# Eight in place of four output tiles scaled by ScalarE and added in DRAM, and a third tile's statistics on ScalarE

## The reference, cut to what matters

```python
x = x + gnn(_layernorm(x), edge_index, W, b)                # 1250 x 1024, 20000 edges
x = x + ffn(_layernorm(x)[None], router_w, ..., ln_w, ln_b)[0]

# inside ffn: hidden_states is the second layer norm's result, 8 experts, 2 of them for each row
for e in range(n_exp):
    y = jax.nn.gelu(flat @ w1[e].T + b1[e], approximate=False)
    y = y @ w2[e].T + b2[e]
    out = out + y * cw[:, None]
out = out.reshape(b, s, h) + hidden_states
return _layernorm(out, ln_w, ln_b)       # (out - mu) * rsqrt(var + 1e-12) * w + b
```

## Time and profile before

| | us |
|---|---|
| median of 3 runs | 693.21 |
| lowest, highest | 691.17, 694.19 |
| time of the profiled execution | 693.42 |
| its span, first to last instruction | 691.7 |
| outside the span | 1.7 |

### The profile page before, as it was taken

The page is one execution under the profiler, slowest core; times in us unless marked ns, Lnnn a source line. Parts: engine busy times, 40 slices in busy tenths (PEclk is TensorE's granted clock), DMA queues, the critical chain, the costliest instruction groups (busy, mean ns, idle before and its releaser), DMA issues.

```text
span 691.7 us, 13064 instructions
## 1 busy us (share of the span) xinstructions
PE 569.9 (82%) x3923; PEld 318.6 (46%) x3924; DVE 495.7 (72%) x1323; ACT 247.5 (36%) x374; POOL 221.8 (32%) x208
## 2 busy tenths in 40 slices
PE   1688999999999999996495999999999988999400
PEld 0243455445444554443383465646565645655100
DVE  8998977776227799999977867675767572363387
ACT  4322433233325234343442434443344341221280
POOL 2730000000000356867636343434343432041231
PEclk9999999999989999999598999999999995999855
DMA  5693000000006423333655787878787878050878
GB/s 197 243 374 122 3 1 1 1 2 2 1 2 231 172 93 147 126 150 122 203 170 181 203 271 179 284 182 281 174 273 184 264 198 309 0 81 13 196 240 262
DMA packets 35052, 106.15 MB, mean 153 GB/s; under 512 B 8978, under 2 KB 9391, under 8 KB 34992
## 3 DMA queue, kind: packets, MB, share of 16 engines
q1 hardware_dynamic: 24912, 73.86, 28.6%
q0 software_dynamic: 8896, 27.38, 18.8%
q10 hardware_dynamic: 1184, 4.20, 2.0%
HBM read 71.75 MB, written 33.67 MB: 152 GB/s over the span
## 4 chain that ended last, share of the span: by engine, by line
PE 55%; DVE 31%; issue 6%; DMA 4%; ACT 1%; DVEq 1%; POOL 1%; POOLq 0%; ACTq 0%; SPq 0%
PE ps L1863 6%; PE ps L1865 6%; PE ps L1864 6%; PE ps L1825 5%; PE ps L1826 5%; PE ps L1827 5%; PE ps L1657 4%; PE ps L1658 3%; PE ps L1659 3%; PE ps L1807 3%; PE ps L1603 2%; DVE last_ends L1328 2%; DVE wbufs L1143 2%; DVE oh_all L1022 2%; DVE wbufs L1246 2%
## 5 line engine op out<-in xcount | busy, mean ns | idle before, releaser
L606 POOL DMA_INDIRECT acc_rows<-work,ids_out x24 | 47.8, 1990 | 134.1 <-DVE work L1464 134.1
L511 POOL TENSOR_TENSOR work<-work 128x1024 f16<-128x1024 f32 x9 | 19.1, 2128 | 217.0 <-ACT work L872 217.0
L1825 PE MATMUL ps<-rows_and_counts,wbufs 128*128 128x336 f16 (+1 forms) x256 | 75.3, 299 | 9.0 <-DVE rows_and_counts L1406 5.6
L1417 DVE SCALAR_TENSOR_TENSOR wbufs<-stage,wbufs 128x1024 f16<-128x1024 f32 x56 | 67.1, 1218 | 12.6 <-ACT wbufs L899 12.6
L1733 PE MATMUL ps<-wbufs,rows_and_counts 128*128 128x512 f16 x200 | 75.8, 379 | 0.5 <-DVE wbufs L1246 0.5
L1734 PE MATMUL ps<-wbufs,rows_and_counts 128*128 128x512 f16 x200 | 75.8, 379 | 0.0
L1826 PE MATMUL ps<-rows_and_counts,wbufs 128*128 128x336 f16 (+1 forms) x256 | 75.3, 299 | 0.0
L1827 PE MATMUL ps<-rows_and_counts,wbufs 128*128 128x336 f16 (+1 forms) x256 | 75.2, 299 | 0.0
L1863 PE MATMUL ps<-wbufs,rows_and_counts 128*128 x192 | 73.4, 382 | 1.4 <-issue 1.4
L1864 PE MATMUL ps<-wbufs,rows_and_counts 128*128 x192 | 73.3, 382 | 0.0
L1865 PE MATMUL ps<-wbufs,rows_and_counts 128*128 x192 | 73.3, 382 | 0.0
(11 more groups left out here) (307 smaller groups left out, 1176.6 us busy)
## 6 DMA issues: line engine op xcount, KB each, us to landing
stage<-wst_in SPq DMA_DIRECT2D x72, 512.0 KB, 6.3
acc_rows<-work SPq DMA_DIRECT2D x10, 512.0 KB, 2.6
x_rows<-work SPq DMA_DIRECT2D x10, 512.0 KB, 2.6
t<-x_in SPq DMA_DIRECT2D x1, 4096.0 KB, 14.1
wbufs<-b_in ACTq DMA_DIRECT2D x8, 512.0 KB, 6.3
wbufs<-acc_rows SPq DMA_DIRECT2D x8, 512.0 KB, 6.2
t<-x_in SPq DMA_DIRECT2D x1, 3072.0 KB, 10.2
t<-x_in SPq DMA_DIRECT2D x1, 2048.0 KB, 7.8
```

The lines of the kernel that those rows point to most:

```text
L1825: mm(o, wbufs[:, ds(w + ws, P)], x_hi, start=(j == 0), stop=False)
```

## The change

Tiles 4 to 7 move from `WHOLE` to `ADDED`, and tile 2 moves from VectorE's statistics to ScalarE's.

```diff
-ACT_TILES = (0, 1), (4, 5), (8,)
-ADDED = LAST_GROUPS[0]
-WHOLE = LAST_GROUPS[1] + LAST_GROUPS[2]
+ACT_TILES = (0, 1, 2), (4, 5), (8,)
+ADDED = LAST_GROUPS[0] + LAST_GROUPS[1]
+WHOLE = LAST_GROUPS[2]
```

## The result

| | before | changed |
|---|---|---|
| median, us | 693.7 (4 runs) | 706.21 (4 runs) |
| lowest to highest, us | 691.17 to 694.43 | 704.0 to 708.72 |
| span of the profiled execution, us | 691.7 | 707.0 |

The ratio is 1.0187, 95% interval 1.0158 to 1.0217: the change costs about 13 us. (Each ratio in this document compares a kernel with runs of the kernel before that were taken together with it.) I had forecast 699.0, with a range up to 702.0. The sign is right; the size is less than half of what was measured, and the time lies outside the range. The changed kernel's profiled execution (708.72) is the highest of its four runs, 2.5 us above their median, so part of what its trace shows over the forecast is its own.

A forecast was written before the change was run, and what follows sets the result against it. The DMA engines were taken to bound the end: full from 671.3 for 23.9 us, to 695.2, plus 2.1 us, span 697.3. That is +5.6 us on 691.7; added to the profiled 693.42 us, 699.0 us, range 696.0 to 702.0.

The forecast's parts named there:

- What bounds the kernel: Last stage: chain of waits runs through VectorE's line 1560 (4.78 us) to the last plain store; full DMA engines then bound.
- both readings: Last stage read by the chain of waits (VectorE's work), and by DMA traffic per stretch (engines full 670.0 to 686.5).
- From the last byte to the end: End of the span: 0.6 us from last byte to landing plus 1.5 us from landing to end, 2.1 us.
- The DMA engines: Last stage: adds take 2.55 us a tile, plain stores 1.27; engines full from 671.3 for 23.9 us, to 695.2.
- The rival in which adds overlap: Last stage: queued adds move over some 240 GB/s, so GpSimd's issues bound; 691.9 to 694.3 us, chance 0.12.
- The third tile: Tile 2's statistics on ScalarE delay the group 0 root, first scaling and first add by 1.30 us, counted in full.
- VectorE's path: Last stage: without line 1560 x4, VectorE ends at 683.5 rather than 687.5; on this path alone a 3.9 us gain.
- GpSimd's issues: Last stage: at 2.2 to 2.3 us each, fifth add starts at 678.3, eighth at 685.2, faster than the DMA engines work.
- The early stores: Four more plain stores of `t`, 5.1 us of data at about 585 to 590, where engines were idle; costed at nothing.
- the rival: At 582 to 590, store traffic holds PE's clock at half speed 5.1 us longer: about 2.5 us, 701.5; chance 0.11.
- The range: Whole kernel time: 696.0 to 702.0 us, taking in the 699.0 forecast and 701.5, 0.86 less some for the runs' spread.

## Why the prediction was wrong, point by point

**What bounds the kernel: the step that failed.** I took the chain of waits as the answer for the kernel before and corrected it only for the DMA engines. In both readings the span of the kernel before ended with the last plain store, and for the changed kernel I hung the same 1.5 us behind the last add. The forecast had the number that should have led on: the fourth add landed at 674.73 + 9.2 = 683.9, and GpSimd waits for it. I did not ask what GpSimd does between that and the end, 7.8 us later. The rows of line 105 answered it in the trace of before.

**From the last byte to the end: mis-sized.** I took 0.6 + 1.5 = 2.1 us: 0.6 us from the engines' last byte to the landing, from the first add, and 1.5 us from the landing to the end, from the last plain store, which SyncE awaits. Even the 1.5 us was no price of the store: SyncE was done 0.2 us after it landed (690.4), and the rest was the wait for GpSimd's drain. Behind an add awaited by GpSimd it is 7.8 us from landing to end, in every kernel where GpSimd waited for its adds. That is 6.3 us of the 9.7 us by which the profiled span (707.0) exceeds the forecast one (697.3). The rest: the first add started 0.2 us late and the DMA engines began on it 0.5 us later than its start plus 1.8 us, because of the longer issue; their work took 25.0 us (672.0 to 697.0) instead of 23.9; and the last landing came 2.2 us after the engines had all but ended (share 0.07), instead of 0.6. 6.3 + 0.2 + 0.5 + 1.1 + 1.6 = 9.7. Why the last add lands so late the runs don't show. Some 2.5 of the 9.7 us may belong to this execution, which was slower than the median by that much; the tail of 7.8 us doesn't, it is the same in the traces of all five kernels whose GpSimd waits for adds.

**The DMA engines: right.** Adds at half the rate of plain stores, no gain from more in the queue (208 GB/s beside 206), the stores in between sharing the engines (271 GB/s while they did), 24 to 25 us of full engines. The rival in which adds overlap fell.

**The third tile: right in the rows.** The root of group 0 came at 662.08 (forecast 661.9), the first scaling at 667.52 (667.34). In the times it is 1 to 2 us, not separable from zero.

**VectorE's path: right.** 4 us sooner, and worth nothing, as forecast. But for the kernel before I had credited this path with the end: it had about 1 us of slack.

**GpSimd's issues: right on the mean.** The eighth started at 685.23 (forecast 685.2). The single issues were 2.62 to 1.55 us, for a reason that I didn't have; that they average to the spacing of before is partly luck.

**The early stores: right.** PE's clock came back in the same place, between 584 and 588 us, with the four more stores still running:

```profile
584.00:586.00 2.00, 2.00 (x9) 1.12 (x8) 0.00 (x0) 0.00 (x0) 0.00 (x0) 0.53 1.03 422
586.00:588.00 2.00, 2.00 (x16) 1.38 (x15) 0.00 (x0) 0.00 (x0) 0.00 (x0) 1.00 1.03 420
```

In the kernel before the stretch from 584 to 586 stood at 0.59. Full clock at a DMA share of 1.03: that clock and traffic changed together in the earlier trace rows was a coincidence, and the rival fell. The first load of the last stage was issued at 645.87 beside 645.70.

**The range.** It was built from rates and starts, and held no term for an end that another engine sets. A range of ±3 us can't cover a missing mechanism of 6 us.

## What to carry to other kernels

Before costing a change at the end of a kernel, list for each engine when its last wait ends and what it still does after it. The chain of waits may stop ahead of that, and an unexplained gap between the last landing and the end of the span is a term like any other. Let an engine whose closing is long (GpSimd here) go first and put the final waits on one whose closing is short. And cost an add in DRAM as two plain stores on the DMA engines (206 beside 413 GB/s here), whatever it takes off a compute engine.

## What the runs showed of the hardware that I had not expected

- GpSimd's drain at the end of the program takes 7.34 to 7.66 us after GpSimd's last wait, with adds, with plain scatters, or with nothing issued for over 30 us; SyncE's takes 7 ns. Entered before the last landing, it ends 4.0 to 4.1 us after it (four kernels). What the drain does in that time the traces don't show.
- A VectorE instruction with two operands in SBUF in many cases stretched the issue of an add that ran beside it from 1.55 to between 1.94 and 2.62 us, and in others didn't; with one of the operands in PSUM it never did.
- Undisturbed, issuing an add takes GpSimd 1.55 to 1.58 us, a plain scatter of the same shape 0.96 to 0.99 us.
